# Writing out every loop of a cross-attention and feed-forward kernel, and moving the normalising of the next batch's first two row tiles

## The reference, cut to what matters

```
kv_c = ctx @ W_kvc                      # 512 x 256 per batch
q_c  = layernorm(x) @ W_dq              # 512 x 384
q, k, v per head (16 heads of 128) from q_c and kv_c, and a rope part of 64
scores = (q k^T + q_rope k_rope^T) / sqrt(192), masked to 9 keys around seg_id
x = x + softmax(scores) @ v, all heads, @ W_o
# feed-forward: one of 64 tiles is chosen for each token
xn = layernorm(layernorm(x)) * gamma + beta
tile_idx = argmax over tiles of sign(xn) against the tile's signature, inside the best cluster
x_slice = the 16 values of xn of that tile; per tile the min and max over all tokens
u = scaled x_slice; out = x + spline(u, bases, slopes) * output_scale, scattered to the 16 places
```

## Time and profile before

| | us |
|---|---|
| median of 3 runs | 3417.23 (3416.03 to 3420.47) |
| the profiled execution's own time | 3417.62 |
| its span, first to last instruction | 3415.9 |
| PE busy with matmuls | 3135.1 (92%) |
| DVE busy | 2099.5 (61%) |
| ACT busy | 1481.1 (43%) |
| POOL busy | 724.8 (21%) |

### The profile page before, as it was taken

The page is one execution under the profiler, slowest core; times in us unless marked ns, Lnnn a source line. Parts: engine busy times, 40 slices in busy tenths (PEclk is TensorE's granted clock), DMA queues, the critical chain, the costliest instruction groups (busy, mean ns, idle before and its releaser), DMA issues.

```text
span 3415.9 us, 49503 instructions
## 1 busy us (share of the span) xinstructions
PE 3135.1 (92%) x13890; PEld 2398.2 (70%) x13890; DVE 2099.5 (61%) x4426; ACT 1481.1 (43%) x2879; POOL 724.8 (21%) x522
## 2 busy tenths in 40 slices
PE   7999799999899998999899998999989999999635
PEld 4788657886688757887578866788568875888522
DVE  2555437775577737766377754767467763777656
ACT  2655425453444425444255533454245452544300
POOL 5222231112211131110311122111311103111126
PEclk9999899999999999999999999999999999999855
DMA  5554444443534435443544444444444434444201
GB/s 199 192 172 172 165 161 136 139 139 125 183 124 138 135 129 180 137 139 118 173 133 137 132 140 170 127 132 132 148 155 139 136 119 162 161 133 135 89 27 3
DMA packets 172396, 475.49 MB, mean 139 GB/s; under 512 B 34385, under 2 KB 65361, under 8 KB 151649
## 3 DMA queue, kind: packets, MB, share of 16 engines
q1 hardware_dynamic: 167184, 472.86, 42.0%
q0 software_dynamic: 5072, 0.88, 0.5%
HBM read 369.57 MB, written 70.52 MB: 129 GB/s over the span
## 4 chain that ended last, share of the span: by engine, by line
PE 71%; DVE 13%; issue 6%; ACT 4%; POOL 3%; DMA 1%; DVEq 1%; SPq 0%; ACTq 0%; POOLq 0%
PE psC L1696 15%; PE psD L1689 9%; PE psA L1629 8%; PE psT L1680 5%; PE psB L1638 4%; PE psA L1598 4%; PE psD L1648 4%; PE psS L1665 3%; PE psS L1671 3%; PE psB L1598 3%; PE psS L1667 3%; PE psS L1668 3%; PE psS L1666 3%; DVE x_slice L1308 2%; ACT exps_ring L947 1%
## 5 line engine op out<-in xcount | busy, mean ns | idle before, releaser
L1696 PE MATMUL psC<-w_o_pair,attn_hi 128*128 128x512 f32 x1920 | 639.6, 414 | 69.8 <-DVE acc L1237 37.2
L947 ACT ACTIVATE exps_ring<-exps_ring,neg_max 128x512 f32<-128x512 f32 x512 | 370.3, 723 | 488.6 <-DVE neg_max L1202 488.1
L1202 DVE CUSTOM_DVE_ANT_0 exps_ring<-psS,mask 128x512 f32<-128x512 f32 x512 | 353.8, 691 | 325.5 <-PE psS L1671 308.0
L958 ACT ACTIVATE probsT_hi<-psT 128x512 fp32r<-128x512 f32 x512 | 304.7, 597 | 384.0 <-PE psT L1680 383.3
L1696 PEld LDWEIGHTS psC<-w_o_pair,attn_hi 128*128 128x128 f32 x1920 | 333.2, 190 | 137.7 <-DVE acc L1237 38.1
L953 ACT ACTIVATE exps_ring<-exps_ring,row_sum_inverse 128x512 f32<-128x512 f32 x512 | 369.4, 722 | 68.6 <-DVE row_sum_inverse L1208 68.2
L1214 DVE TENSOR_TENSOR probsT_lo<-psT,probsT_hi 128x512 fp32r<-128x512 f32 x512 | 350.5, 686 | 61.8 <-ACT probsT_hi L958 59.9
L1696 PE MATMUL psC<-w_o_pair,attn_lo 128*128 128x512 f32 x960 | 380.5, 396 | 0.0
L1230 DVE TENSOR_TENSOR acc<-acc,psC 128x512 f32<-128x512 f32 x448 | 305.6, 682 | 28.6 <-PE psC L1696 25.2
L1680 PE MATMUL psT<-ident,exps_ring 128*128 128x128 f32 x2048 | 305.4, 272 | 2.0 <-ACT exps_ring L953 2.0
L1680 PEld LDWEIGHTS psT<-ident,exps_ring 128*128 128x128 f32 x2048 | 253.6, 140 | 68.1 <-ACT exps_ring L953 2.4
(11 more groups left out here) (224 smaller groups left out, 5542.2 us busy)
## 6 DMA issues: line engine op xcount, KB each, us to landing
w_o_pair<-w_o_split SPq DMA_DIRECT2D x112, 1024.0 KB, 5.3
w_uq_ring<-w_uq_split SPq DMA_DIRECT2D x112, 384.0 KB, 3.7
w_uk_ring<-w_uk_split SPq DMA_DIRECT2D x112, 256.0 KB, 2.7
w_uv_quad<-w_uv_split SPq DMA_DIRECT2D x28, 1024.0 KB, 4.9
w_qr_sorted<-w_qr_split SPq DMA_DIRECT2D x28, 768.0 KB, 4.6
x_stage<-in_x_dram SPq DMA_DIRECT2D x32, 512.0 KB, 5.3
x_stage<-in_ctx_dram SPq DMA_DIRECT2D x32, 512.0 KB, 3.4
acc<-in_x_dram SPq DMA_DIRECT2D x32, 512.0 KB, 5.6
```

The source lines that it names most:

```text
L947: act.activation(E[:, qt, :], E[:, qt, :], ACT.Exp, scale=-1.0, bias=mx[:, i % 2, qt:qt + 1], accum_out=rs[:, i % 2, qt:qt + 1]).then_inc( ...
L958: act.activation(PT[0][:, :, qt * P:(qt + 1) * P], psT[qt % 2][:, :].rearrange("p (c n) -> p c n", c=TT), ACT.Copy)\
L1202: dve.tensor_tensor_reduce(E[:, qt, :], psS[qt % 2][:, :], mask[:, qt, :], -SCALE, BIG, ALU.add, ALU.min, mx[:, i % 2, qt:qt + 1]).then_in ...
L1696: mm_ = pe.matmul(ps[:, :], attn[a][:, 2 * pair + i, t * P:(t + 1) * P], WO[:, half, o, i, :], start=i + a + o == 0, stop=i + a == 2)
```

## The change

It does two things.

1. All loops are written out. The batch loop and the quad loop of every engine become Python loops, so `b` and `q` are plain numbers everywhere, no branch is left inside the work, and every semaphore is compared with a constant. `wait_apart` goes, and so do its increments. The tests `isinstance(q, int) and q == 0`, which told the written-out quad from the looped one, become `q == 0`; they select the same branches as before.
2. In batches 1 to 6 the next batch's row tiles 0 and 1 are normalised in quads 1 and 2. Row tile `q - 1` has its `norm_stats` in head 1, step 3, of quad `q`, and its `norm_x` in head 2, step 2. POOL's `rstds` moves with them, behind `ffn_sums` of that quad.

```diff
-        def batches(eng, body):
-
-            body(0, True, False)
-            with eng.Fori(1, B - 1) as b:
-                body(b, False, False)
-            body(B - 1, False, True)
+        def batches(body):
+
+            for b in range(B):
+                body(b, b == 0, b == B - 1)
...
# on SP, POOL, ACT, DVE and PE alike
-                with dve.Fori(1, NQ) as q:
+                for q in range(1, NQ):
...
# each wait_apart(eng, ...) of SP, POOL and DVE
-                wait_apart(dve, s_S, n + 1)
+                dve.wait_ge(s_S, n + 1)
...
# POOL, the feed-forward part of a quad
-                def ffn(q, rows=False):
+                def ffn(q):
                     ffn_rstds(b - 1, q)
-                    if rows:
-                        rstds(b + 1, [0])
                     ffn_sums(b - 1, q, fsel)
+                    if not last and 1 <= q <= 2:
+                        rstds(b + 1, [q - 1])
                     ffn_select(b - 1, q)
-                    if rows:
-                        rstds(b + 1, [1])
...
# DVE, body
                 ffn = steps(0)
-                if not first and not last:
-                    rows = [[lambda: norm_stats(b + 1, 0), lambda: norm_x(b + 1, 0)],
-                            [lambda: norm_stats(b + 1, 1), lambda: norm_x(b + 1, 1)]]
-                    for step, part in zip((6, 7, 10, 11), rows[0] + rows[1]):
-                        ffn[step // TT][step % TT].append(part)
                 for i in range(HQ - 1):
                     head(0, i, True, None, ffn)
-                with dve.Fori(1, NQ) as q:
+                for q in range(1, NQ):
                     head(q - 1, HQ - 1, False, q, steps(q - 1))
                     ffn = steps(q)
+                    if not first and not last and 1 <= q <= 2:
+                        t = q - 1
+                        ffn[1][3].append(lambda: norm_stats(b + 1, t))
+                        ffn[2][2].append(lambda: norm_x(b + 1, t))
                     for i in range(HQ - 1):
                         head(q, i, False, None, ffn)
...
-def wait_apart(eng, sem, n):
-
-
-    eng.wait_ge(sem, n)
-    if not isinstance(n, int):
-        eng.sem_inc(WAITS_APART[0], 1)
```

More of the change, by code:

```diff
@@ L52, in pos_a @@
     def pos_a(b, q, k):
[L53 removed]
+        if q == 0 and k == 0:
             return b * AN + 2
@@ L796, in body @@
                 else:
-                    ffn(0, not last)
-                with pool.Fori(1, NQ) as q:
+                    ffn(0)
+                for q in range(1, NQ):
                     rope_lo(b, q)
@@ L853, in stage_turned @@
                     act.wait_ge(fullT, b * TN + k + 1)
-                    if k == 0 and not (isinstance(b, int) and b <= 1):
+                    if k == 0 and not (b <= 1):
                         act.wait_ge(s_f, (b - 1) * TT * NF)
@@ L920, in q_hi @@
                 act.wait_ge(fullA, pos_a(b, q, 1 + i) + 1)
-                if not (isinstance(q, int) and q == 0 and i == 0):
+                if not (q == 0 and i == 0):
                     act.wait_ge(s_S, tile_no(b, q, i, 0))
@@ L1079, in body @@
                     head(0, i, True)
-                with act.Fori(1, NQ) as q:
+                for q in range(1, NQ):
                     head(q - 1, HQ - 1, False, q)
@@ L1116, in norm_stats @@
                 dve.wait_ge(s_xs[t % 2], 16 * (b * TT + t // 2 + 1))
-                if not (isinstance(b, int) and b == 0 and t == 0):
+                if not (b == 0 and t == 0):
                     dve.wait_ge(s_ln, (b * TT + t) * NL)
@@ L1157, in rope_q @@
                 c = Chain(dve, s_rope, rope_base(b, q))
-                if not (isinstance(n, int) and n == 0):
+                if not (n == 0):
                     dve.wait_ge(s_rope, rope_base(b, q))
@@ L1258, in norm @@
                     dve.wait_ge(s_rstd2, 2 * k + 1)
-                    if not (isinstance(k, int) and k == 0):
+                    if not (k == 0):
                         dve.wait_ge(s_z, z_before(k))
@@ L1582, in turn_stage @@
                         pe.wait_ge(freeT, b * TN + k - 1)
-                    elif not (isinstance(b, int) and b == 0):
+                    elif not (b == 0):
                         pe.wait_ge(s_ptlo, b * H * TT - 1 + k)
@@ L1676, in turn_probs @@
                 pe.wait_ge(s_prob, n + 1)
-                if not (isinstance(n, int) and n < 2):
+                if not (n < 2):
                     pe.wait_ge(s_ptlo, n - 1)
@@ L1809, in body @@
                     head(0, i, True)
-                with pe.Fori(1, NQ) as q:
+                for q in range(1, NQ):
                     rope_queries(b, q)
```

222 lines of the change are left out of this document (109 added, 113 removed).

## The result

| | us |
|---|---|
| before, median of the runs beside it | 3416.63 |
| changed, median of 4 runs | 3330.2 (3329.1 to 3332.53) |
| ratio, with its 95% interval | 0.9747 (0.973 to 0.9764) |
| the changed kernel's profiled execution | 3331.05 |
| its span | 3329.2 |

The kernel is 86.4 us faster, against a forecast of 68.9. The measured 3330.2 lies 4 us under the low end of the range, 3334. The span fell by 3415.9 - 3329.2 = 86.7 us, and that number is taken apart here. The last two kernels of this text each had one run of over 10 ms, which is left out.

The account below looks back on a forecast made before the run. TensorE, busy for 92% of the span, was taken as the bound, so only its idle time could be won. Terms 44.5 + 7.7 + 1.0 + 0 + 12.6 + 3.1 = 68.9 us less gave 3349 us, range 3334 to 3384.

Parts of the forecast that it names:

- Part 1, quad 0: Quad 0 of batches 1 to 6: becomes what batch 7's is, 65.07 us each, 44.5 us less in all.
- The pause: Start of batches 2 to 6: TensorE's pause assumed to bring the clock dips; 7.9 us lost if the dips stayed.
- Part 2, quads 1 to 3: Quads 1 to 3 of batches 1 to 6: without register arithmetic they reach batch 7's 227.43 us, 7.7 us less.
- 0.5 us each: Batches 0 and 7: gain when their own quad loops are written out, 1.0 us together.
- Part 3, the tiles in quads 1 and 2 at nothing: Row tiles moved to quads 1 and 2: VectorE's added work unseen by TensorE, cost nothing; other end 32 us.
- Part 4, the boundaries: Between batches: 12.6 us less without five branches back, 3.1 less without registers, nothing ahead of the down-projection.
- its split: Boundaries from the down-projection on: five branches back 12.6 us, registers 3.1 us (0.51 in each of six).
- the 96 to 97 that it named as its sign: Boundaries of 96 to 97 us, with a microsecond's pause ahead of the first scores, would show part 4 right.
- The tiles did not take their price along: Rival, 12%: moved tiles make quads 1 and 2 grow by 5.4 us a batch, 32.4 in all: 3381 us.
- The dips did not stay: Rival, 8% together with the load of x: clock dips stay in quad 0, +7.9 us, 3357 us.
- The load of the next x: Rival, 8% together with the dips: this load slows quad 0, which stays near 71.16 us; 36.5 lost, 3385 us.
- The third rival: Rival, 3%: straight code cannot be fetched fast enough, about 128 packets in 32 quads, 124 us on top: 3473 us.

Follow-up runs that it names:

- The last two kernels of this text: The changed kernel with TensorE's quad loop kept in batch 0 alone, 3335.8 us, and with it kept in batches 1 to 7 alone, 3327.27 us.
- the kernel beside it: The changed kernel with TensorE's quad loop kept in batch 0 alone and written out in batches 1 to 7: 3335.8 us, ratio 0.9761.

## Why the forecast was right in kind and short in size

**Part 1, quad 0: right, 2.2 us short.** The forecast had "these quads become what batch 7's is", at 65.07 us, and they became 64.65 to 64.71. Batch 7 itself went to 64.67. The stretch ends at head 4, and head 3 is the first one inside the quad loop; in batch 7 it went from 18.5 to 18.0 us, and that is the 0.4 us, six times. The pause does bring the slow clock, as the kernel with a pause and no branch shows. What the forecast left open is why quad 0 was late. It put the tiles, the waits and the jump into one term, and the only branch that it read was TensorE's; VectorE's does not occur in it. With all other loops out, the tiles cost 3.0 us a batch, VectorE's registers 1.4 and its branch back 4.7. These prices cannot be added: put back one at a time, the tiles cost 21 us of the whole, TensorE's batch loop 33, VectorE's 45 and the other engines' loops 7, which makes 106, and all of it together cost 86. So they hide behind each other in part; that this is because several waits end at one matmul is my reading, and no run tested a pair of them. Batch 7's row was free of all of them at once, and so the term came out nearly right without its parts being known.

**Part 2, quads 1 to 3: 3.0 us short.** The same row again: "Batch 7, whose quad loop has registers of `q` alone" was taken as the end, 227.43 us. The forecast then gave batches 0 and 7 0.5 us each for those registers, and forgot them in the six batches between. They are the missing 227.43 - 226.95 = 0.48 us, six times 0.48 is 2.9. The size of 0.5 is itself a balance. In the kernel of the move alone, with VectorE's and GpSimd's quad loops out and TensorE's kept, batch 7 takes 226.36 us, 1.1 less than before; in the changed kernel it takes 226.87. And batch 0, which was to gain 0.5 us here too, went from 226.65 to 227.09.

**Part 3, the tiles in quads 1 and 2 at nothing: right.** Quads 1 and 2 take 83.0 us with and without them.

**Part 4, the boundaries: 7.6 us short, and this is the step that failed.** For the part ahead of the down-projection it says: "between 0 and 1 us a boundary, I take nothing." That part lost 1.3 us in each of the six boundaries, 7.8 us in all, above even the 1 us it allowed. With VectorE's batch loop put back alone, 0.9 of the 1.3 come back, so VectorE's register arithmetic is most of it. There was no row of the same code without registers, and "no counterpart" was turned into nothing, though quads 1 to 3 had just shown that registers cost. Behind the down-projection the forecast was right in sum, 15.5 us against 15.7, but its split is not borne out: batch 6, without a branch back, lost 0.1 us there and not 0.51. And the boundaries are at 94.7 to 95.7 us, below the 96 to 97 that it named as its sign.

**Batch 0's boundary: 5.0 us that had no term.** The sum left that stretch out. The forecast looked at batch 0's loop only for what it costs inside the quads. Three of the five microseconds are shown to be the price of TensorE's quad loop there, by two kernels that differ in where that loop is kept. That it acts through the packet brought at its exit is what fifteen traces agree on, not an edit by itself. The other two microseconds stay open. The packet of queue 14 is a candidate, and so is the clock, which was at 0.50 for 27.3 us of that boundary before and is for 17.1 now; no run tried either.

**The rivals.** The tiles did not take their price along. The dips did not stay. The load of the next x is still there, and quad 0 is at 64.7 us. Straight code was brought in: 114 packets of queue 8 and "issue" at half its share. The third rival's price is not zero, though. The kernel with TensorE's quad loops in batches 1 to 7 brings 71 packets on queue 8 in place of 114, and its batches 1 to 6 take 386.15 us on average. In the kernel beside it, where they are straight, they take 387.14, and in the two traces of the changed kernel 386.77 and 386.87. So straight code costs TensorE 0.6 to 1.0 us a batch here, with the loop's own registers already set against it.

The Trainium skill (Runtime: NRT & Kernel Launch, "Instruction fetch mechanics") says that a taken branch outside the window held costs a fetch before execution goes on. The traces agree: TensorE stands still for 3.1 to 3.8 us at a branch back, with two packets on queue 8, and VectorE for 3.2 us, with one on queue 14 (whose code that queue brings, no view says). It also says that crossing a block in straight code is mostly hidden. That agrees as well, with the 0.6 to 1.0 us a batch above for what is not.

## What to carry to other kernels

Count the loops of every engine, not only of the one that bounds. VectorE's batch loop was the dearest here, 45 us, about half in its branches back (4.7 us each) and half in its registers, though VectorE was busy for 61% of the time. TensorE's cost 33 us, nearly all of it branches back (6.6 us each with the slow clock behind them). A stretch of the same program that runs without a cost is the best price for taking it away, better than a sum of its parts; where no such stretch exists, carry over the nearest price rather than nothing. And straight code is not best everywhere: a short loop on TensorE saved up to another microsecond a batch, if its exit does not fall among large loads.

## What the runs showed of the hardware that was not expected

- VectorE idles for 3.22 us behind a branch back whose own row is 68 ns long; on TensorE the branch's row is 4.9 to 5.5 us long, and matmuls pause for 3.1 to 3.8 us.
- A wait of 4.2 us for data puts the granted clock to 0.50, the 1.2 GHz level, for 3.4 or 6.8 us, five times of five. Waits of 2.9 us did it six times of seven. The waits of 2.4 us for `q_lo` in the kernel before have a dip behind them once in six batches.
- One packet of instructions among saturated loads: two loads of 512 KB take 9.4 us in place of 7.4. Why is open.
